# Chunks 0 and 1 of a feed-forward stage: other order of VectorE and ScalarE work, other PSUM banks for the first transposed x, two memsets earlier

## The chip, the core and the metric

The kernel runs on one core of a Trainium2 chip. Five engines share the work: TensorE (PE in the rows, its weight loads PEld), VectorE (DVE), ScalarE (ACT), GpSimd (POOL) and SyncE (SP), which issues every DMA here. Each works through its own instructions in order and waits on semaphores. The metric is the device time of one execution in microseconds (us), lower is better. Before the change it is 366.3 us, the median of three runs (364.39 to 366.59).

## What is computed

For x of shape (16, 256, 256) in float32:

```python
xn = _layernorm(x, axis=-1)
x = x + _L0_attn_ref(xn, w_qkv, w_out) + _L0_ffn_ref(xn, w_gating, w_linear)

# _L0_ffn_ref: every product takes float8 (e4m3) inputs
ff_gate = _qdot(x, w_gating[0])          # 256 -> 1024
gate_value = jax.nn.gelu(ff_gate)
ff1 = _qdot(x, w_gating[1])
activations = gate_value * ff1
outputs = _qdot(activations, w_linear)   # 1024 -> 256
```

The attention has 16 heads of 16, a causal mask and softmax, in float32.

## The kernel before

The 4096 rows of x are worked as 8 chunks of 512 tokens in a feed-forward (FFN) stage, about the first 110 us; after it a long attention stage runs over the 16 batches. In the profile of the kernel before the FFN of chunk c, called "chunk c" here, starts on TensorE at 10.78 us for chunk 0, then at 25.53, 37.76, 49.50 and 61.25 us for the chunks 1 to 4.

Layernorm of a chunk: VectorE takes statistics of four tiles (`find_stats`, L369), joins them (`aggregate`, L378), GpSimd raises the variance to the power -1/2 (`find_rstd`, L288 and L290), VectorE writes the normalised tiles `xn` (`normalize`, L387, four of 128x256). `xn` is a single buffer. TensorE transposes it (`transpose_x`, L661, twice four of 128x128) into two PSUM banks `xt_ps`. ScalarE reads each bank twice: `cast_xt` (L516) makes the fp8 input `x8` of the products, `round_xt` (L521) the high float32r part of a copy that attention needs. VectorE subtracts the two (`split_xt`, L394) for the low part. SyncE then stores both parts, the tile `xt_part`, to memory (`store_xt`, L188, two DMAs of 512 KB). `xt_part` is a single buffer too, so `round_xt` of chunk c waits on the semaphore `xt_stored` until the stores of chunk c-1 have landed.

The FFN of a chunk has eight steps j. A step is two fp8 matmuls for the gate (L676) and two for the up product (L682), the gelu on ScalarE (L527) and the product of both on VectorE (`activate`, L423). The gate of step j waits for the gelu of step j-2, the up product for the activate of step j-2, since both have two banks. Between the steps of chunk c, TensorE computes a piece of the down product of chunk c-1 (`down`, L697); the first piece of chunk 0 waits for all eight activates and for four casts of `w_linear`.

The weights arrive as float32 by DMA into `arena` and are cast to fp8: the first half of the columns of `w_gating` in one VectorE cast (L406), the second half by VectorE (up, L431) and ScalarE (gate, L596, 1024 elements), `w_linear` (`wl8`) in four ScalarE casts (L600). GpSimd also clears two constants for attention (L300, L301), scales the query weights (`w_raw`, L310), and adds the FFN output to x (`add_ffn`, L298).

What stands between the steps on each engine is written out by hand as conditions on (c, j) in one loop per engine. SyncE issues in order: `store_xt(0)`, then the loads of the attention weights (L193, L194) and of further x (L168), then `store_xt(1)` and so on.

## Time and profile before

| what | value |
|---|---|
| median of three runs | 366.3 us |
| the profiled execution | 366.19 us |
| its span, first to last instruction | 364.5 us |
| TensorE busy | 341.3 us (94%) |
| VectorE busy | 298.5 us (82%) |
| ScalarE busy | 227.6 us (62%) |
| GpSimd busy | 168.2 us (46%) |
| TensorE's share of the chain that ended last | 81% |
| mean granted TensorE clock | 0.972 of 2.4 GHz |

The span leaves out 1.7 us ahead of the first and behind the last instruction. Busy shares are means over stages that differ; the change touches only work between 0 and some 50 us, so those stretches have to be read by themselves. Times in rows are us from the span's start.

### The profile page before, as it was taken

The numbers are of one execution on the slowest core, as the hardware profiler recorded it, in microseconds if no ns is written. First come the engines' busy times: TensorE is split into PE (matmuls) and PEld (weight loads), VectorE is DVE, ScalarE is ACT, GpSimd is POOL, SyncE is SP. The second block draws the span as 40 slices with busy tenths as digits, with TensorE's granted clock in tenths as the row PEclk, the third lists the DMA queues.
The fourth block names the chain that finished last, engine by engine and source line by source line (L and its number), as shares of the span: only waits on it lengthen the run. The fifth ranks groups of instructions, "written<-read, shape, count | busy, mean of one in ns | idle before, by whom it ended". The sixth has DMA issues, their size and how long they took to land.

```text
span 364.5 us, 9751 instructions
## 1 busy us (share of the span) xinstructions
PE 341.3 (94%) x3498; PEld 260.1 (71%) x3498; DVE 298.5 (82%) x1356; ACT 227.6 (62%) x368; POOL 168.2 (46%) x204
## 2 busy tenths in 40 slices
PE   7789999999999789999999999999999999979775
PEld 6336565666677678788788888888887888866454
DVE  5968988998425678999989999999999899996643
ACT  1655786667655376776676767766766767664540
POOL 2212333232235137456665575475566555753441
PEclk9969999999999999999999999999999999995889
DMA  7987655773248242534637528447355373250001
GB/s 251 323 287 224 183 151 141 175 232 123 77 142 298 65 145 90 201 120 150 193 112 225 167 97 263 120 144 246 104 179 195 112 222 118 91 206 30 32 29 59
DMA packets 46553, 57.59 MB, mean 158 GB/s; under 512 B 2664, under 2 KB 39080, under 8 KB 46504
## 3 DMA queue, kind: packets, MB, share of 16 engines
q1 hardware_dynamic: 46504, 56.96, 48.6%
q8 instruction: 28, 0.46, 0.5%
q14 instruction: 21, 0.17, 0.1%
HBM read 16.78 MB, written 12.58 MB: 81 GB/s over the span
## 4 chain that ended last, share of the span: by engine, by line
PE 81%; DVE 10%; ACT 3%; issue 2%; DMA 2%; SPq 0%; POOL 0%; DVEq 0%; ACTq 0%; POOLq 0%
PE ps L805 13%; PE ps L710 12%; PE ps L786 12%; PE ps L765 9%; PE ps L717 7%; PE ps L697 6%; PE ps L676 6%; PE ps L822 6%; PE ps L682 6%; DVE masked L457 3%; PE ps L814 2%; DMA xres<-in_L_attn_x_dram 2%; PE ps L661 2%; ACT arena L572 2%; DVE act L423 1%
## 5 line engine op out<-in xcount | busy, mean ns | idle before, releaser
L457 DVE CUSTOM_DVE_ANT_0 masked<-ps,causal 128x256 bf16<-128x256 f32 (+1 forms) x512 | 148.5, 353 | 21.1 <-PE ps L765 21.1
L572 ACT ACTIVATE arena<-ps 128x1024 f32<-128x1024 f32 x96 | 98.4, 1025 | 61.1 <-PE ps L786 61.0
L330 POOL TENSOR_SCALAR_AFFINE_SELECT arena<-arena 128x512 f32<-128x512 f32 (+1 forms) x96 | 73.6, 787 | 39.1 <-ACT arena L572 38.9
L304 POOL TENSOR_TENSOR qk_part<-w_raw,qk_part 128x512 fp32r<-128x512 f32 x32 | 41.1, 1286 | 55.5 <-ACT qk_part L551 55.5
L527 ACT ACTIVATE gate<-ps 128x512 bf16<-128x512 f32 x64 | 38.5, 602 | 35.0 <-PE ps L676 32.6
L786 PE MATMUL ps<-stack 64*128 64x256 f32 (+1 forms) x512 | 53.0, 307 | 4.8 <-ACT arena L572 4.8
L805 PE MATMUL ps<-arena,v_aug 128*32 128x256 f32 (+1 forms) x1024 | 50.8, 341 | 2.9 <-DVE o_norm L474 2.8
L710 PE MATMUL ps<-xs,wq_part 128*128 128x256 f32 x384 | 52.3, 285 | 0.3 <-ACT w_raw L545 0.3
L765 PE MATMUL ps<-stack 63*128 63x256 f32 (+1 forms) x512 | 48.3, 288 | 3.2 <-DVE row_max L457 3.1
L786 PEld LDWEIGHTS ps<-stack 64*128 64x128 f32 x512 | 36.9, 190 | 18.7 <-issue 7.3
L710 PEld LDWEIGHTS ps<-xs,wq_part 128*128 128x128 f32 x384 | 47.5, 189 | 1.6 <-ACT w_raw L545 0.6
L805 PEld LDWEIGHTS ps<-arena,v_aug 128*32 128x32 f32 x1024 | 30.1, 113 | 19.4 <-issue 6.0
L457 DVE DVE_READ_ACCUMULATOR2_ANT row_max<- 128x1 f32 x512 | 42.3, 83 | 0.0
L765 PEld LDWEIGHTS ps<-stack 63*128 63x128 f32 x512 | 37.4, 191 | 6.9 <-DVE row_max L457 2.4
L298 POOL TENSOR_TENSOR xres<-xres,ffn 128x512 f32<-128x512 f32 x16 | 18.5, 1154 | 37.6 <-ACT ffn L533 37.6
L423 DVE TENSOR_TENSOR arena<-ps,gate 128x512 fp8e4<-128x512 f32 x32 | 22.0, 686 | 16.0 <-ACT gate L527 15.9
L335 POOL TENSOR_TENSOR xt_part<-xn,xt_part 128x256 fp32r<-128x256 f32 x32 | 23.4, 731 | 22.9 <-ACT xt_part L581 22.9
L822 PE MATMUL ps<-wq_part,xt_part 128*128 128x256 f32 x192 | 31.4, 302 | 1.0 <-DVE w_raw L487 1.0
L466 DVE STREAM_TRANSPOSE ps<-ps 128x512 f32<-128x512 f32 x32 | 23.4, 731 | 8.0 <-PE ps L805 8.0
L822 PEld LDWEIGHTS ps<-wq_part,xt_part 128*128 128x128 f32 x192 | 25.5, 195 | 3.8 <-DVE w_raw L487 1.2
L423 DVE TENSOR_TENSOR act<-ps,gate 128x512 fp8e4<-128x512 f32 x32 | 21.9, 684 | 7.2 <-ACT gate L527 4.4
L717 PE MATMUL ps<-wq_part,xs 128*128 128x256 f32 x192 | 26.7, 288 | 0.0
(60 smaller groups left out, 458.6 us busy)
## 6 DMA issues: line engine op xcount, KB each, us to landing
stack<-qk_part SPq DMA_DIRECT2D x96, 256.0 KB, 2.7
xt_store<-xt_part SPq DMA_DIRECT2D x16, 512.0 KB, 4.2
xs<-xt_store SPq DMA_DIRECT2D x16, 512.0 KB, 4.2
out_dram<-w_raw SPq DMA_DIRECT2D x16, 256.0 KB, 4.1
xres<-in_L_attn_x_dram SPq DMA_DIRECT2D x7, 512.0 KB, 6.7
arena<-in_L_ffn_w_gating_dram SPq DMA_DIRECT2D x2, 1024.0 KB, 8.9
stack<-zeros SPq DMA_DIRECT2D x4, 512.0 KB, 7.5
arena<-in_L_ffn_w_linear_dram SPq DMA_DIRECT2D x1, 1024.0 KB, 12.9
```

The lines of the kernel that those rows point to most:

```text
L304: nc.gpsimd.tensor_tensor(qk_part[:, g, QLO:KLO + 1:3, :], qk_raw[:, g, :, :], qk_part[:, g, QHI:KLO, :].bitcast(F32), ALU.subtract).then_ ...
L330: nc.gpsimd.affine_select(diag, diag, pattern=[[0, 1024 // width], [1, P]], compare_op=ALU.is_ge, fill=0.0, base=0, channel_multiplier=-1) ...
L423: nc.vector.tensor_tensor(act8[c % 2][:, j, :], up_ps[j % 2], gate[:, j % 2, :], ALU.mult, saturate=False).then_inc(act_done, 1)
L457: last = nc.vector.tensor_tensor_reduce(masked[:, place, i * width:(i + 1) * width], max_ps[:, place, i * width:(i + 1) * width], causal[: ...
L527: nc.scalar.activation(gate[:, j % 2, :], gate_ps[j % 2], ACT.Gelu_apprx_tanh).then_inc(gelu_done, 1)
L572: nc.scalar.activation(arena[:, n, :, :], exp_ps, ACT.Exp).then_inc(exp_done, 1)
L710: last = nc.tensor.matmul(misc[:, 1, s * S:(s + 1) * S], wq_part[:, a, kt, col:col + P], xs[b % 2][:, z, kt, :], start=(i == 0), stop=(i = ...
L717: last = nc.tensor.matmul(misc[:, 0, t * D:(t + 1) * D], xs[b % 2][:, z, kt, t * P:(t + 1) * P], wq_part[:, a, kt, 2 * D:3 * D], start=(i ...
L765: last = nc.tensor.matmul(max_ps[:, (2 * unit + u) % 3, i * width:(i + 1) * width], st[rows, j0 + i, 0, qt * P:(qt + 1) * P], st[rows, j0 ...
L786: last = nc.tensor.matmul(exp_ps[:, u, i * width:(i + 1) * width], st[rows, j0 + i, 1, kt * P:(kt + 1) * P], st[rows, j0 + i, 0, kt * P:S] ...
L805: last = nc.tensor.matmul(pv_ps[32 * i:32 * i + 32, u * S + kt * P:(u + 1) * S], va[:, kt, 2 * (HG * c + i) + u, :], cols, start=(kt == 0) ...
L822: last = nc.tensor.matmul(misc[:, 0, t * D:(t + 1) * D], ot_part[:, z, c, t * P:(t + 1) * P], wq_part[:, a, c, 3 * D:4 * D], start=(c == t ...
```

## The change

Seven things are altered, all of them around chunks 0 and 1, with a tail in chunk 2:

1. GpSimd clears `zeros` and `v_aug2` before `find_rstd(0)` instead of after `find_rstd(1)`.
2. The first half of `w_gating` is cast by VectorE in two pieces of 256 columns, and the gate of step 2 waits for the second; ScalarE's part of the second half is cast in two pieces of 512 elements, after steps 1 and 2 instead of all after step 1.
3. The transposed x of chunk 0 goes to `exp_ps`, the banks of the down product. The transposes of chunk 1 therefore no longer wait for `split_xt` of chunk 0, and the first down piece does.
4. VectorE in chunk 0: `aggregate(1)` after step 0, its weight cast after step 1, `normalize(1)` in pairs after steps 2 and 3, `split_xt(0)` after steps 4 and 5; `find_stats(2)` and `aggregate(2)` leave chunk 0 for chunk 1.
5. ScalarE in chunk 0: `round_xt(0)` after steps 0 and 3, `cast_xt(1)` after 5 and 6, `w_linear` casts after 3, 4 and two after 7; `round_xt(1)` moves into chunk 1, after its steps 0 and 1.
6. Chunk 1: `normalize(2)` after steps 3 and 4 (before: 0 to 3), the transposes of chunk 2 after the down pieces of steps 5 and 6 (before: 4 and 5), `cast_xt(2)` after 6 and 7; the second halves of `round_xt(2)` and `split_xt(2)` fall into chunk 2.
7. TensorE transposes chunk 1 in one go after step 5 of chunk 0 (before: after 4 and 5).

From chunk 3 on nothing is altered. The core of the diff:

```diff
+            nc.gpsimd.memset(zeros[:, :], 0.0).then_inc(v_ones, 1)
+            nc.gpsimd.memset(v_aug[2][:, :, :, :], 1.0).then_inc(v_ones, 1)
             find_rstd(0)
             find_rstd(1)
...
-            nc.gpsimd.memset(zeros[:, :], 0.0).then_inc(v_ones, 1)
-            nc.gpsimd.memset(v_aug[2][:, :, :, :], 1.0).then_inc(v_ones, 1)
...
+                    if c == 0:
+                        if j == 0:
+                            aggregate(1)
+                        if j == 1:
+                            half = slice(HID // 2, HID)
+                            dve.wait_ge(wg_in[1], 16)
+                            nc.vector.tensor_copy(wg8[:, 1, :, half], wg_raw[:, 1, :, half], saturate=False).then_inc(wg_cast[1], 1)
+                        if j in (2, 3):
+                            normalize(1, 2 * j - 4)
+                            normalize(1, 2 * j - 3)
+                        if j in (4, 5):
+                            split_xt(0, j - 4)
+                        continue
+                    if c == 1:
+                        if j in (0, 1):
+                            find_stats(2, 2 * j)
+                            find_stats(2, 2 * j + 1)
+                        if j == 1:
+                            aggregate(2)
+                        if j == 2:
+                            for k in range(KD):
+                                split_xt(1, k)
+                        if j in (3, 4):
+                            normalize(2, 2 * j - 6)
+                            normalize(2, 2 * j - 5)
...
+                        if j == 7:
+                            aggregate(3)
+                            split_xt(2, 0)
+                        continue
+                    if c == 2 and j == 0:
+                        split_xt(2, 1)
...
+                    if c == 1 and j in (0, 1):
+                        round_xt(1, j)
+                    if c == 1 and j in (6, 7):
+                        cast_xt(2, j - 6)
+                    if c == 1 and j == 7:
+                        round_xt(2, 0)
+                    if c == 2 and j == 0:
+                        round_xt(2, 1)
...
-                if c >= 1:
+                if c >= 2:
                     pe.wait_ge(xt_lo, KD * (c - 1) + k + 1)
...
+                if c == 0 and j == J // 4:
+                    pe.wait_ge(wg_cast[0], 2)
```

How the rows stand in the engines' programs is shown at two places. First ScalarE around the border of chunks 0 and 1, from the gelu of step 5 of chunk 0 (before) and from the same step (after). `CAST arena<-ps` is `cast_xt(1)`, `CAST xt_part` is `round_xt`, `CAST wl` the weight cast, `ACTIVATE gate` the gelu. Before:

```order
L527 ACTIVATE gate<-ps 128x512 [waits act_done,gate_ready]
L600 CAST wl<-arena 128x512 [waits wl_in]
L516 CAST arena<-ps 128x512 [waits xt_ready]
L527 ACTIVATE gate<-ps 128x512 [waits act_done,gate_ready]
L600 CAST wl<-arena 128x512 [waits wl_in]
L516 CAST arena<-ps 128x512 [waits xt_ready]
L521 CAST xt_part<-ps 128x512 [waits xt_stored]
L527 ACTIVATE gate<-ps 128x512 [waits act_done,gate_ready]
L600 CAST wl<-arena 128x512 [waits wl_in]
L521 CAST xt_part<-ps 128x512
```

After:

```order
L559 ACTIVATE gate<-ps 128x512 [waits act_done,gate_ready]
L548 CAST arena<-ps 128x512 [waits xt_ready]
L559 ACTIVATE gate<-ps 128x512 [waits act_done,gate_ready]
L548 CAST arena<-ps 128x512 [waits xt_ready]
L559 ACTIVATE gate<-ps 128x512 [waits act_done,gate_ready]
L634 CAST wl<-arena 128x512 [waits wl_in] x2
L559 ACTIVATE gate<-ps 128x512 [waits act_done,gate_ready]
L553 CAST xt_part<-ps 128x512 [waits xt_stored]
L559 ACTIVATE gate<-ps 128x512 [waits act_done,gate_ready]
L553 CAST xt_part<-ps 128x512
```

The cast that waits on `xt_stored` moved from behind step 6 of chunk 0 to behind step 0 of chunk 1; the next gelu in the queue behind it is now that of step 1 of chunk 1.

Second VectorE at the same border, from the activate of step 7 of chunk 0. `TENSOR_TENSOR act` and `arena` are activates, `xt_part` is `split_xt`, `TENSOR_SCALAR xn` is `normalize`. Before:

```order
L423 TENSOR_TENSOR act<-ps,gate 128x512 [waits up_ready,gelu_done]
L394 TENSOR_TENSOR xt_part<-ps,xt_part 128x512 [waits xt_hi]
L423 TENSOR_TENSOR arena<-ps,gate 128x512 [waits up_ready,gelu_done]
L387 TENSOR_SCALAR xn<-xres,mean_var,rstd 128x256 [waits xt_ready,rstd_done]
L423 TENSOR_TENSOR arena<-ps,gate 128x512 [waits up_ready,gelu_done]
L387 TENSOR_SCALAR xn<-xres,mean_var,rstd 128x256
L423 TENSOR_TENSOR arena<-ps,gate 128x512 [waits up_ready,gelu_done]
L387 TENSOR_SCALAR xn<-xres,mean_var,rstd 128x256
```

After, from the activate of step 0 of chunk 1:

```order
L427 TENSOR_TENSOR arena<-ps,gate 128x512 [waits up_ready,gelu_done]
L373 BN_STATS stats<-xres 128x6 [waits x_in1]
L373 BN_STATS stats<-xres 128x6
L427 TENSOR_TENSOR arena<-ps,gate 128x512 [waits up_ready,gelu_done]
L373 BN_STATS stats<-xres 128x6 x2
L382 BN_AGGR mean_var<-stats 128x2 [waits stats_step]
L382 BN_AGGR mean_var<-stats 128x2 x3
L427 TENSOR_TENSOR arena<-ps,gate 128x512 [waits up_ready,gelu_done]
L398 TENSOR_TENSOR xt_part<-ps,xt_part 128x512 [waits xt_hi] x2
L427 TENSOR_TENSOR arena<-ps,gate 128x512 [waits up_ready,gelu_done]
L391 TENSOR_SCALAR xn<-xres,mean_var,rstd 128x256 [waits xt_ready,rstd_done]
L391 TENSOR_SCALAR xn<-xres,mean_var,rstd 128x256
```

The statistics of chunk 2 and their aggregate now stand in chunk 1, ahead of its normalize, which starts behind step 3 instead of step 0.

## Rows read from the trace of the kernel before

**Rows 1.** The profile page: its first line.

```profile
span 364.5 us, 9751 instructions
```

**Rows 2.** Busy time of each engine by stretch, with granted TensorE clock and DMA share.

```profile
core 0: us, PE busy (x) PEld busy (x) DVE busy (x) ACT busy (x) POOL busy (x), PEclk, DMA share, GB/s
10.78:25.53 14.75, 11.46 (x42) 4.85 (x40) 11.58 (x30) 8.43 (x16) 2.43 (x4) 0.77 0.90 289
25.53:37.76 12.23, 11.46 (x72) 7.07 (x73) 9.97 (x24) 8.33 (x17) 4.13 (x5) 1.00 0.77 227
37.76:49.50 11.74, 11.61 (x74) 7.00 (x72) 10.80 (x25) 8.62 (x18) 3.56 (x5) 1.00 0.64 181
61.25:97.00 35.75, 35.75 (x226) 21.66 (x223) 31.13 (x66) 25.34 (x50) 10.50 (x12) 1.00 0.47 135
```

**Rows 3.** Timeline of TensorE: start, duration, line, operation, [idle before, releaser].

```profile
10.78 0.59 PE L676 MATMUL ps<-x,wg 128*128 128x512 fp8e4 x2
11.21 0.59 PE L682 MATMUL ps<-x,wg 128*128 128x512 fp8e4 x2
...
15.96 0.60 PE L682 MATMUL ps<-x,wg 128*128 128x512 fp8e4 x2 [1.81 <-DVE act L423]
...
19.32 1.12 PE L661 MATMUL ps<-ident,xn 128*128 128x128 f32 x4 [0.80 <-DVE xn L387]
...
25.53 0.60 PE L676 MATMUL ps<-arena,wg 128*128 128x512 fp8e4 x2 [0.17 <-ACT arena L516]
...
32.99 0.60 PE L661 MATMUL ps<-ident,xn 128*128 128x128 f32 x4
```

**Rows 4.** Timeline of VectorE in chunk 0.

```profile
13.32 0.69 DVE L431 CAST wg<-arena 128x1024 fp8e4<-128x1024 f32 x1 [0.27 <-DMA arena<-in_L_ffn_w_gating_dram]
14.09 1.22 DVE L387 TENSOR_SCALAR xn<-xres,mean_var,rstd 128x256 f32<-128x256 f32 x1
...
17.34 0.68 DVE L394 TENSOR_TENSOR xt_part<-ps,xt_part 128x512 fp32r<-128x512 f32 x1
17.94 0.40 DVE L387 TENSOR_SCALAR xn<-xres,mean_var,rstd 128x256 f32<-128x256 f32 x1
18.26 0.68 DVE L423 TENSOR_TENSOR act<-ps,gate 128x512 fp8e4<-128x512 f32 x1
```

**Rows 5.** Timeline of ScalarE in chunk 0.

```profile
18.01 0.61 ACT L600 CAST wl<-arena 128x512 fp8e4<-128x512 f32 x1
...
25.36 0.60 ACT L521 CAST xt_part<-ps 128x512 fp32r<-128x512 f32 x1
25.84 0.62 ACT L527 ACTIVATE gate<-ps 128x512 bf16<-128x512 f32 x1
```

**Rows 6.** Timeline of GpSimd.

```profile
14.22 0.94 POOL L301 MEMSET v_aug<- 128x1024 f32 x1
...
26.05 1.04 POOL L290 TENSOR_TENSOR rstd<-var_eps,minus_half 128x4 f32<-128x4 f32 x1
27.19 1.51 POOL L310 TENSOR_SCALAR w_raw<-w_raw 128x512 f32<-128x512 f32 x1
33.48 1.15 POOL L298 TENSOR_TENSOR xres<-xres,ffn 128x512 f32<-128x512 f32 x1 [4.78 <-ACT ffn L533]
```

**Rows 7.** Timeline of SyncE's queue, two rows.

```profile
3.40 0.74 SPq L181 DMA_DIRECT2D arena<-in_L_ffn_w_linear_dram  x1
...
18.05 1.31 SPq L188 DMA_DIRECT2D xt_store<-xt_part  x2
```

**Rows 8.** DMA: page (last number: us to landing); chunk 0's two stores, from issue.

```profile
arena<-in_L_ffn_w_linear_dram SPq DMA_DIRECT2D x1, 1024.0 KB, 12.9
...
DMA to landing us min/median/max: 3.4/4.1/4.8
```

**Rows 9.** Busy time by stretch, the columns of rows 2: around the fall of the clock.

```profile
13.10:17.48 4.38, 2.07 (x9) 0.62 (x9) 4.09 (x7) 2.40 (x4) 2.06 (x3) 0.98 0.99 315
17.50:24.00 6.50, 5.70 (x17) 2.88 (x18) 4.37 (x10) 2.81 (x6) 0.00 (x0) 0.50 0.75 229
```

More of the change, by code:

```diff
@@ L404, in _ @@
             dve.wait_ge(wg_in[0], 16)
-            half = slice(0, HID // 2)
-            nc.vector.tensor_copy(wg8[:, :, :, half], wg_raw[:, :, :, half], saturate=False).then_inc(wg_cast[0], 1)
+            for i in range(2):
+                cols = slice(i * HID // 4, (i + 1) * HID // 4)
+                nc.vector.tensor_copy(wg8[:, :, :, cols], wg_raw[:, :, :, cols], saturate=False).then_inc(wg_cast[0], 1)
             for i in range(CT):
                 find_stats(1, i)
-            aggregate(1)
             def split_wq(i, k):
@@ L590, in _ @@
                     gelu(c, j)
[L591 to L593 removed]
+                    if c == 0 and j in (0, 3):
+                        round_xt(0, j // 3)
+                    if c == 0 and j in (1, 2):
                         half = slice(HID // 2, HID)
                         act.wait_ge(wg_in[1], 16)
[L596 to L598 removed]
+                        nc.scalar.copy(wg8[:, 0, j - 1, half], wg_raw[:, 0, j - 1, half], saturate=False).then_inc(wg_cast[1], 1)
+                    if c == 0 and j in (5, 6):
+                        cast_xt(1, j - 5)
+                    for i in {(0, 3): (0,), (0, 4): (1,), (0, 7): (2, 3)}.get((c, j), ()):
+                        rows = slice(2 * i, 2 * i + 2)
                         act.wait_ge(wl_in, 16)
                         nc.scalar.copy(wl8[:, rows, :], wl_raw[:, rows, :], saturate=False).then_inc(wl_cast, 1)
+                    if c == 1 and j in (0, 1):
[6 more added lines that the diff above has]
+                        round_xt(2, 1)
                     if c >= 2 and j == 0:
@@ L692, in down @@
                         pe.wait_ge(wl_cast, J // 2)
+                        pe.wait_ge(xt_lo, KD)
                 if piece % 4 == 0 and c >= 1:
```

40 lines of the change are left out of this document (19 added, 21 removed).

## Prediction

> **What bounds the kernel now.** I read the stretches first. The span is 364.5 us [rows 1] of the execution's 366.19, so 1.69 us lie outside it; the execution is 0.1 us under the median of 366.3. From chunk 4 on TensorE is busy 35.75 of 35.75 us at the full clock [rows 2]: there its own matmuls are the bound, and any time that TensorE wins or loses in chunks 0 to 2 is carried to the end unchanged. Chunk 1 takes 12.23 us with 11.46 busy, chunk 2 11.74 with 11.61, so 0.8 us of idle time is all that those two hold. Chunk 0 takes 14.75 us with a mean clock of 0.77 [rows 2]. Its work is short: the matmuls for one gate or one up product start 0.43 us apart (10.78 and 11.21 [rows 3]), eight steps are 7.0 us, with the two transposes 7.8. So chunk 0 holds about 7 us that are not TensorE's own.
>
> Then the timeline of TensorE. It sits idle 1.81 us before 15.96 and 0.80 us before 19.32 [rows 3], behind VectorE. VectorE's first normalize of chunk 1 takes 1.22 us at 14.09 [rows 4] against 0.40 for one at 17.94; it ends at 15.31, just after GpSimd's memset of 14.22 + 0.94 = 15.16 [rows 6]. Of the stretch 13.10 to 17.48 TensorE is busy 2.07 us out of 4.38, and in 17.50 to 24.00 the granted clock is 0.50, the lower level of 1.2 GHz [rows 9].
>
> **The change, step by step.** I carry the new orders forward with the spacings of the rows: on ScalarE a gelu or cast starts 0.48 us after the one before it (25.36, 25.84 [rows 5]), a weight cast about the same; on VectorE an activate or split takes 0.60 and a normalize 0.32 (17.34, 17.94, 18.26 [rows 4]); a result is used about 0.04 us after it is there.
>
> Chunk 0. The memsets, now ahead of the first rstd, run while VectorE awaits x; nothing waits for them. If they delayed VectorE's own memsets, the cost is 0 to 0.6 us at the start, and it would vanish in the two DMA waits below; I take 0. TensorE starts at 10.78 as before. The activate of step 1 no longer stands behind rstd(1), so steps 0 to 3 run without a stall until 14.2. The second half of `w_gating` lands at 13.3 (VectorE's cast at 13.32 [rows 4]), ScalarE's two pieces end about 15.0, and step 4 starts there. `w_linear` was issued at 3.40 [rows 7] and takes 12.9 us to land [rows 8]: 16.3. ScalarE now wants it at 15.8 (before: at 18.01 [rows 5]), a stall of 0.5, so the gelu of step 4 starts at 16.9. From there ScalarE does four gelus (steps 4 to 7), two `cast_xt` and three weight casts, nine times about 0.49: the gelu of step 0 of chunk 1 starts at 21.3 (before: 25.84 [rows 5]). TensorE transposes chunk 1 at 17.1 (before 19.32 [rows 3]), at the full clock, and opens chunk 1 at 20.0 (before 25.53 [rows 3]). Chunk 0 has won 5.6 us.
>
> The new wait. `split_xt(0)` has moved from steps 1 and 2 to steps 4 and 5 of VectorE. Before, its second half ended at 17.34 + 0.68 = 18.02, and SyncE issued the two stores at 18.05, 1.31 us together [rows 7]. Now: gelu 4 at 16.9, activate 4 at 17.5, split 18.1, activate 5 at 18.7, split 19.3 to 20.0. SyncE issues at 20.05 and 20.7, and the later store lands 4.8 us after its issue [rows 8]: 25.5. Before, that was 23.5, and `round_xt(1)` came only at 25.36 [rows 5], so it waited for nothing. Now ScalarE reaches `round_xt(1)` at 21.8, right behind its first gelu of chunk 1, and stands until 25.6: 3.8 us. Behind it in ScalarE's queue is the gelu of step 1, now at 26.1, behind that the activate of step 1 (26.8) and, by the two gate banks, TensorE's gate of step 3. TensorE computes steps 0 to 2 and is idle from 24.5 to 26.8. Before, step 3 lay two steps of 1.30 (gate, up, down piece, 0.43 each) ahead of the transposes at 32.99 [rows 3], at 30.4, so 3.6 us of the lead are still there.
>
> The late statistics. Only behind the activate of step 1 do the last statistics and `aggregate(2)` follow: they end at 28.6, and GpSimd's two steps (0.3 and 1.04 [rows 6]) give rstd(2) at 30.1 (before 26.05 + 1.04 = 27.1). VectorE comes to `normalize(2)` behind the activate of step 3 at 30.9. GpSimd then scales `w_raw`, 1.51 us from 30.0, and adds the FFN result, 1.15 us [rows 6], since copy_ffn is done by 30.3; the weights for the scaling are there at 29.2 (27.19 less 18.05 [rows 6, 7] behind the new issue at 20.05). These two ran at 27.19 and 33.48, clear of each other. Rows 4 show what a normalize does beside GpSimd: it ended 0.15 us behind a memset that started after it, so it was held over two GpSimd instructions. So the first normalize of chunk 2 ends at 32.8, the last at 34.4, with the activate of step 4 between, and the transposes of chunk 2, at 32.99 before [rows 3], start at 34.4, 1.4 us later. TensorE is idle from 32.0 to 34.4. This port has a rule: the Trainium skill, page SBUF — State Buffer, section SBUF: two separate sides, has VectorE and GpSimd share one pair of ports under an exclusive lock, held for one whole instruction by whoever starts first. By it normalize could slip in between the scaling and the addition; the transposes would start near 34.1 and the sum below would be 0.3 us less. The row with 1.22 us speaks for the longer hold.
>
> Then less is left to do than before at that point, as the transposes stand a step later: one of them, two steps, two down pieces, the other, 3.5 us, but `cast_xt(2)` comes only after the gelu of step 7, and chunk 2 opens at 38.4 instead of 37.76 [rows 2]: 0.6 us late. In chunk 2 the second `split_xt(2)` stands ahead of the first normalize of chunk 3, 0.6 us more on VectorE; TensorE's wait for that chunk's `xn`, small before (chunk 2 held 0.13 us idle [rows 2]), grows by 0.5. Together +1.1 us. From chunk 3 all is as before.
>
> The clock. TensorE is busy 3.9 us (at full speed) out of the 9.9 between 24.5 and 34.4, less than the 2.07 of 4.38 behind which it fell to 1.2 GHz before [rows 9]. A fall is likely. Where it costs is open: the low level began near 17.3 (the mean of 0.98 up to 17.48 leaves 0.2 us for it) and held at least to 24.0 [rows 9], some 7 us; between 24.5 and 34.4 TensorE waits for others and half speed hides; dense work behind 34.4 pays half of the low time. Lower end 0, if it recovers by 34.4; upper end 3.5 if all 7 us fall behind it. By the nearest row, the fall came about 1.3 us after the end of the idle time (15.96 to 17.3): here 28.1 to 35.1, so 0.7 us of dense work at half speed, a loss of 0.35. I take +0.4.
>
> Sum: 366.2 + 0.6 + 0.5 + 0.4 = 367.7 us. The low clock of chunk 0, 7 us long, is gone, but it wins nothing more: its end lay ahead of the store's landing.
>
> **Rivals.** (a) The clock falls late: the same stalls, but TensorE pays 1.2 to 3.5 us of it behind 34.4: 368.5 to 370.8. For it: two idle stretches of 2.3 us and the second right ahead of dense work. Against it: one fall may be over by then. It decides from 34.4 us on. (b) The store is early enough. Were xt_stored there when ScalarE comes, chunk 1 would shift by 2.6 us: 366.2 - 1.5 = 364.7. For it: the first of the two stores took 3.4 us, not 4.8 [rows 8]; a landing 1.1 us sooner would already give 366.7. Against it: the wait needs the second store as well. More than 3.7 us, a gain of over 1%, asks that also rstd(2) and the normalizes come free of GpSimd, for which no row speaks: chunk 2 would open near 34. (c) The losses cancel the gain to within 0.7 us: chunk 1 is bound by its own chain (statistics, rstd, normalize), and a few tenths less there (the port, rule above) end at 366.2.
>
> **Numbers.** My case, 367.0 to 368.5: 0.42. Rival (a): 0.25. (b): 0.17. (c): 0.16. The range must hold 0.8: from 364.6, the fully hidden wait, to 370.4, most of (a). This kernel's measurement tells about 1% (3.7 us) from no change. Slower by more than that (over 370.0) is the upper part of (a), 0.13 with what is unforeseen; faster (under 362.6) is the far end of (b), 0.05; within 1% 0.82.
>
> **What would show it.** In the profile of the changed kernel: TensorE's gates of step 3 at about 13.4 without idle time, opening chunk 1 at about 20; ScalarE idle some 3.8 us in front of the `round_xt` of chunk 1, ended by a DMA, near 25.6; VectorE's first normalize of chunk 2 near 31 with over 1 us duration; TensorE idle twice over 2 us between 24 and 35; chunk 2 opening at 38 to 39. Wrong would be: no ScalarE stall there, or a chunk 2 that opens before 36.5; and a granted clock of 0.5 behind 35 us would move the result to (a).

## The result, and the profile after

| | before | after |
|---|---|---|
| median | 365.25 us (6 executions, 361.95 to 366.59) | 368.59 us (6 executions, 366.66 to 370.12) |
| profiled execution | 366.19 us | 367.46 us |
| span | 364.5 us | 365.7 us |
| mean granted TensorE clock | 0.972 | 0.981 |

The ratio of after to before is 1.0087, with a 95% interval of 1.0051 to 1.0122: the change makes the kernel some 3 us slower. A few executions of a kernel run one or two per cent slower at a lower granted clock; the ratios here and below leave them out and are worked out from all the others, so they are not exactly the quotients of the medians. The predicted time was 367.7 us in a range of 364.6 to 370.4.

The page of the changed kernel, its first two lines and the chain that ended last:

```profile
span 365.7 us, 9753 instructions
...
PE 340.6 (93%) x3498; PEld 258.6 (71%) x3498; DVE 297.9 (81%) x1357; ACT 227.5 (62%) x369; POOL 169.0 (46%) x204
...
PE 73%; DVE 12%; DMA 5%; issue 4%; ACT 3%; SPq 1%; POOL 1%; DVEq 0%; ACTq 0%
```

The chain of the kernel before:

```profile
PE 81%; DVE 10%; ACT 3%; issue 2%; DMA 2%; SPq 0%; POOL 0%; DVEq 0%; ACTq 0%; POOLq 0%
```

No engine has more or less to do. What changed is the chain: TensorE's share fell from 81% to 73%, and that of DMAs rose from 2% to 5%. Where that lies, the stretches show; the first three are the chunks 0, 1 and 2, the fourth is as long as the last one of [rows 2], and the last two are cut around TensorE's waits:

```profile
core 0: us, PE busy (x) PEld busy (x) DVE busy (x) ACT busy (x) POOL busy (x), PEclk, DMA share, GB/s
10.96:21.02 10.06, 8.72 (x40) 3.46 (x41) 9.06 (x23) 7.81 (x16) 1.83 (x2) 1.00 0.78 263
21.02:38.87 17.85, 14.03 (x74) 7.24 (x73) 12.29 (x29) 8.42 (x17) 3.97 (x4) 0.90 0.78 247
38.87:51.11 12.24, 11.54 (x73) 7.00 (x74) 11.19 (x29) 8.87 (x18) 3.99 (x5) 1.00 0.76 201
62.85:98.60 35.75, 35.75 (x226) 21.67 (x223) 31.12 (x66) 25.39 (x50) 10.49 (x12) 1.00 0.46 135
24.00:28.00 4.00, 1.91 (x14) 1.09 (x12) 0.52 (x3) 1.26 (x3) 0.00 (x0) 1.00 0.93 288
28.80:32.00 3.20, 3.20 (x11) 1.47 (x10) 2.86 (x10) 1.28 (x4) 1.63 (x3) 0.50 0.63 219
```

Against [rows 2], chunk 0 takes 10.06 us instead of 14.75, chunk 1 17.85 instead of 12.23, chunk 2 12.24 instead of 11.74, and the dense chunks the same 35.75. Chunk 1 opens 4.51 us earlier than before and gives 5.62 us back, so chunk 2 opens 1.11 late and chunk 3 1.61 (51.11 against 49.50). Chunk 0 now runs at the full clock; the low level of 1.2 GHz is found from 28.8 to 32.0.

Then TensorE's timeline, to set beside [rows 3]:

```profile
10.96 0.60 PE L720 MATMUL ps<-x,wg 128*128 128x512 fp8e4 x2
...
13.72 0.60 PE L726 MATMUL ps<-x,wg 128*128 128x512 fp8e4 x2 [0.42 <-DVE act L427]
...
16.06 0.60 PE L720 MATMUL ps<-x,wg 128*128 128x512 fp8e4 x2 [0.87 <-ACT wg L628]
...
21.02 0.60 PE L720 MATMUL ps<-arena,wg 128*128 128x512 fp8e4 x2
...
27.88 0.60 PE L720 MATMUL ps<-arena,wg 128*128 128x512 fp8e4 x2 [2.09 <-ACT gate L559]
...
34.87 0.66 PE L703 MATMUL ps<-ident,xn 128*128 128x128 f32 x4 [0.95 <-DVE xn L391]
...
38.87 0.60 PE L720 MATMUL ps<-x,wg 128*128 128x512 fp8e4 x2 [0.30 <-ACT x L548]
...
46.28 0.66 PE L703 MATMUL ps<-ident,xn 128*128 128x128 f32 x4 [0.70 <-DVE xn L391]
```

The two long waits for VectorE in chunk 0 (1.81 and 0.80 in [rows 3]) are gone; the up product of step 2 still waits 0.42 us, and the gate of step 4 waits 0.87 us for ScalarE's cast. In chunk 1 there are two new ones: 2.09 us until the gelu of step 1 frees a gate bank, and 0.95 us for `xn` of chunk 2. The last row is the wait for `xn` of chunk 3, which chunk 2 did not show before.

ScalarE, against [rows 5], and the two stores in SyncE's queue with their landing, against [rows 7, 8]:

```profile
14.38 0.62 ACT L628 CAST wg<-arena 128x512 fp8e4<-128x512 f32 x1 [1.19 <-DMA arena<-in_L_ffn_w_gating_dram]
...
17.39 0.62 ACT L634 CAST wl<-arena 128x512 fp8e4<-128x512 f32 x1 [0.41 <-DMA arena<-in_L_ffn_w_linear_dram]
...
26.74 0.59 ACT L553 CAST xt_part<-ps 128x512 fp32r<-128x512 f32 x1 [3.75 <-DMA xt_store<-xt_part]
27.22 0.60 ACT L559 ACTIVATE gate<-ps 128x512 bf16<-128x512 f32 x1
```

```profile
21.05 2.61 SPq L192 DMA_DIRECT2D xt_store<-xt_part  x2
...
DMA to landing us min/median/max: 4.2/4.6/5.0
```

ScalarE stands 3.75 us in front of the `round_xt` of chunk 1, where before it waited for nothing. The gelu at 27.22 is the one that TensorE's row at 27.88 names. VectorE and GpSimd, against [rows 4, 6]:

```profile
20.34 0.68 DVE L398 TENSOR_TENSOR xt_part<-ps,xt_part 128x512 fp32r<-128x512 f32 x1
...
27.86 0.69 DVE L427 TENSOR_TENSOR arena<-ps,gate 128x512 fp8e4<-128x512 f32 x1 [3.48 <-ACT gate L559]
...
32.33 1.01 DVE L391 TENSOR_SCALAR xn<-xres,mean_var,rstd 128x256 f32<-128x256 f32 x2
...
33.86 0.96 DVE L391 TENSOR_SCALAR xn<-xres,mean_var,rstd 128x256 f32<-128x256 f32 x2
...
45.82 0.40 DVE L391 TENSOR_SCALAR xn<-xres,mean_var,rstd 128x256 f32<-128x256 f32 x1
```

```profile
30.51 1.04 POOL L294 TENSOR_TENSOR rstd<-var_eps,minus_half 128x4 f32<-128x4 f32 x1
31.64 1.56 POOL L314 TENSOR_SCALAR w_raw<-w_raw 128x512 f32<-128x512 f32 x1
33.17 1.18 POOL L304 TENSOR_TENSOR xres<-xres,ffn 128x512 f32<-128x512 f32 x1
...
45.86 1.38 POOL L304 TENSOR_TENSOR xres<-xres,ffn 128x512 f32<-128x512 f32 x1 [3.56 <-ACT ffn L565]
```

The chain of waits between 20 and 40 us puts these rows in one line; its columns are start, duration, and what it was:

```profile
20.34 0.69 DVE xt_part L398
...
21.05 0.64 SPq L192
...
21.73 4.98 DMA xt_store<-xt_part
...
27.22 0.61 ACT gate L559
...
27.86 0.69 DVE arena L427
...
32.33 1.01 DVE xn L391 x2
...
34.87 0.66 PE ps L703 x4
```

Read downwards: the second `split_xt(0)`, the issue of the second store, its flight of 4.98 us, the gelu that stood behind `round_xt`, VectorE's activate, statistics and normalizes of chunk 2, and only then TensorE. From 26.7 to 34.8 nothing in this chain is TensorE's.

### The profile page after: what moved, and what is told of

It is laid out like the page before. It is cut to its first block, busy times and chain, and to the rows that moved or that the text cites. A ratio compares the mean times of both kernels' runs of the same rounds, so it can differ in the third digit from the quotient of the medians.

```text
span 365.7 us, 9753 instructions
## 1 busy us (share of the span) xinstructions
PE 340.6 (93%) x3498; PEld 258.6 (71%) x3498; DVE 297.9 (81%) x1357; ACT 227.5 (62%) x369; POOL 169.0 (46%) x204
## 4 chain that ended last, share of the span: by engine, by line
PE 73%; DVE 12%; DMA 5%; issue 4%; ACT 3%; SPq 1%; POOL 1%; DVEq 0%; ACTq 0%
PE ps L856 12%; PE ps L756 12%; PE ps L837 11%; PE ps L816 8%; PE ps L763 6%; PE ps L743 5%; PE ps L720 5%; PE ps L873 5%; PE ps L726 4%; DVE masked L489 4%; DMA xres<-in_L_attn_x_dram 3%; PE ps L865 2%; ACT arena L604 2%; PE ps L703 2%; DVE xn L391 2%
## 5 line engine op out<-in xcount | busy, mean ns | idle before, releaser
L756 PE MATMUL ps<-xs,wq_part 128*128 128x256 f32 x384 | 53.4, 289 | 0.3 <-ACT w_raw L577 0.3
L756 PEld LDWEIGHTS ps<-xs,wq_part 128*128 128x128 f32 x384 | 48.5, 192 | 1.6 <-ACT w_raw L577 0.6
L873 PE MATMUL ps<-wq_part,xt_part 128*128 128x256 f32 x192 | 30.5, 296 | 1.0 <-DVE w_raw L519 1.0
L873 PEld LDWEIGHTS ps<-wq_part,xt_part 128*128 128x128 f32 x192 | 24.6, 189 | 3.7 <-DVE w_raw L519 1.2
L763 PE MATMUL ps<-wq_part,xs 128*128 128x256 f32 x192 | 26.7, 288 | 0.0
```

The lines of the kernel that those rows point to most:

```text
L756: last = nc.tensor.matmul(misc[:, 1, s * S:(s + 1) * S], wq_part[:, a, kt, col:col + P], xs[b % 2][:, z, kt, :], start=(i == 0), stop=(i = ...
L763: last = nc.tensor.matmul(misc[:, 0, t * D:(t + 1) * D], xs[b % 2][:, z, kt, t * P:(t + 1) * P], wq_part[:, a, kt, 2 * D:3 * D], start=(i ...
L873: last = nc.tensor.matmul(misc[:, 0, t * D:(t + 1) * D], ot_part[:, z, c, t * P:(t + 1) * P], wq_part[:, a, c, 3 * D:4 * D], start=(c == t ...
```

## The experiments

Two theories stood at the start. The first: chunk 0's gain is real, and the wait of ScalarE for the store of `xt_part` takes it away. The rival: chunk 1 is bound by its own chain of statistics, rstd and normalize, with GpSimd's two instructions beside it, so that the store only looks guilty. Every kernel below computes the whole reference. Ratios are to the kernel before, timed on the same chip; "opens" is the first gate of a chunk on TensorE in the profiled execution, in us. Chips differ: the median of the kernel before was 365.43 for the kernels e, 365.55 for f, 365.82 for g and 365.88 for h1, so kernels of different letters are compared by their ratios. This is the table of all of them:

| kernel | chunk 1 opens | chunk 2 | chunk 3 | median us | ratio [95%] |
|---|---|---|---|---|---|
| before | 25.53 | 37.76 | 49.50 | 365.25 | 1 |
| after | 21.02 | 38.87 | 51.11 | 368.59 | 1.0087 [1.0051, 1.0122] |
| e0_after_again | 20.74 | 40.07 | 52.31 | 369.67 | 1.0139 [1.0091, 1.0186] |
| e1_buffer | 20.73 | 34.47 | 46.71 | 363.91 | 0.9974 [0.9944, 1.0005] |
| e2_scale_waits | 20.80 | 39.48 | 51.72 | 369.25 | 1.0114 [1.0070, 1.0158] |
| e3_buffer_scale_waits | 21.09 | 34.82 | 47.07 | 364.25 | 0.9974 [0.9944, 1.0003] |
| f1_split_early | 20.61 | 37.18 | 50.36 | 367.53 | 1.0040 [1.0012, 1.0068] |
| f2_split_late | 20.82 | 40.39 | 52.64 | 370.29 | 1.0119 [1.0080, 1.0157] |
| f3_round_late | 21.15 | 35.69 | 48.87 | 367.44 | 1.0048 [1.0015, 1.0082] |
| f4_before_memsets | 22.53 | 34.94 | 46.68 | 365.04 | 0.9974 [0.9943, 1.0005] |
| g1_memsets_back | 21.72 | 39.23 | 52.41 | 370.48 | 1.0140 [1.0096, 1.0185] |
| g2_buffer_old_banks | 22.52 | 36.78 | 49.96 | 369.65 | 1.0104 [1.0044, 1.0163] |
| g3_before_again | 26.14 | 38.37 | 50.12 | 366.36, one execution | none |
| h1_buffer_pool_waits | 20.41 | 34.16 | 45.70 | 362.72 | 0.9918 [0.9882, 0.9955] |

One caution for reading it: from the first gate of chunk 7 to the end, where all these kernels are alike, the profiled executions take between 268.0 and 270.7 us of their spans, so a single span is uncertain by over 1 us in either direction. The openings tell where time goes, the medians tell how much is left at the end. The two do not agree in size: e1, e3 and f4 open chunk 3 2.79, 2.43 and 2.82 us before the kernel before does, and their ratio of 0.9974 is 1.0 us; the changed kernel opens it 1.61 us late and is 3 us slower. In every row the ratio lies 0.6 to 3.3 us above what the openings say, and why is not shown.

**The changed kernel once more.** No edit; it is the base for its neighbours on that chip.

> The changed kernel unaltered, beside the three edits of it that follow, for comparison on one chip. All theories: the ratio to the kernel before lies in the interval measured, 1.005 to 1.012, and ScalarE stands some 3.8 us in front of the first round_xt of chunk 1.

Measured: ratio 1.0139, above the interval of the first measurement, though the two intervals overlap. ScalarE's row and the landing of the two stores:

```profile
27.95 0.59 ACT L553 CAST xt_part<-ps 128x512 fp32r<-128x512 f32 x1 [5.24 <-DMA xt_store<-xt_part]
...
DMA to landing us min/median/max: 3.3/4.9/6.5
```

The stores were issued at 20.78, 0.27 earlier than in the first profile, yet the later one landed 6.5 us after its issue instead of 5.0. The stall is 5.24 us and chunk 2 opens 1.20 us later. The length of the stall differs from one execution of the same program to the next.

**A second buffer.** The transposed x of chunk 1 goes to memory that lies unused then, so its `round_xt` need not await chunk 0's store; order and work are those of the changed kernel.

```diff
+        xt_spare = stack[3][:, :, :, :].rearrange("p j a s -> p (j a s)")[:, 0:2 * KD * C].rearrange("p (a k t) -> p a k t", a=2, k=KD)
+
+        def xt_of(c):
+            return xt_spare if c == 1 else xt_part
...
-                if c >= 1 and k == 0:
+                if c >= 2 and k == 0:
...
-                nc.scalar.copy(xt_part[:, 0, k, :], xt_ps(c, k)).then_inc(xt_hi, 1)
+                nc.scalar.copy(xt_of(c)[:, 0, k, :], xt_ps(c, k)).then_inc(xt_hi, 1)
```

> The changed kernel with a second buffer for the xt_part of chunk 1 (it lies in stack[3], unused until much later), so that round_xt(1) needs no wait for the stores of chunk 0. Theory S (the store's landing): ScalarE's 3.8 us of waiting are gone, TensorE's gate of step 3 of chunk 1 comes 2.1 to 2.3 us earlier, the transposes of chunk 2 2.6 us earlier, and the time falls by 2.6 us against the changed kernel, ratio to before about 1.002 or a bit below. Theory P (GpSimd's scaling and addition beside normalize, with the late statistics): chunk 1 ends no earlier, since rstd(2) and the port hold it; ratio stays near 1.009. Theory C (a late fall of the clock costs most): the idle 2.1 us of TensorE at 25.8 are gone, so the fall is rarer; a gain too, but the profile would show the low clock in the changed kernel behind 35 us and not here.

Measured: 363.91 us against 369.67 on the same chip, 5.8 us less, and 0.9974 of before, with an interval that reaches 1.0005: level with it or a little faster. The gain is over twice the 2.6 us expected. Rows of ScalarE, VectorE and TensorE:

```profile
22.54 0.63 ACT L559 CAST stack<-ps 128x512 fp32r<-128x512 f32 x1
...
28.45 0.73 DVE L397 TENSOR_SCALAR xn<-xres,mean_var,rstd 128x256 f32<-128x256 f32 x2
...
34.47 0.60 PE L726 MATMUL ps<-x,wg 128*128 128x512 fp8e4 x2 [0.30 <-ACT x L554]
```

The cast that came at 26.74 or 27.95 comes at 22.54, without a wait, and chunk 2 opens 4.4 us earlier than in the first profile of the changed kernel and 5.6 earlier than in the second. From the opening of chunk 1 to that of chunk 2 it takes 13.74 us, where those two took 17.85 and 19.33: 4.11 and 5.59 less, each time the stall (3.75 and 5.24) and 0.35 us more, and the first pair of normalizes takes 0.73 instead of 1.01. So the wait for the store is the cause, and chunk 1 pays its full length. The stall itself grew between the forecast (3.8) and this comparison (5.24); the forecast of 2.6 had also let the stall move what follows by less than its length.

**GpSimd out of the way.** The scaling of the query weights waits for the last normalize of chunk 2, first in the changed kernel, then in the one with the second buffer.

```diff
+                    pool.wait_ge(xn_done, 3)
                     pool.wait_ge(wq_in, 32)
```

> The changed kernel; GpSimd waits for the last normalize of chunk 2 before it scales the query weights, so that neither this nor the addition behind it runs beside a normalize of chunk 2. Theory S: 1.5 us of the loss at most are the port's, since the first two normalizes took 1.01 us and the other two 0.96 where a pair takes 0.72 alone: by those rows 0.5 us less, by the prediction's own working (held over both instructions) 1.5 us; ratio 1.004 to 1.008. Theory P: the port is the larger part, 1.5 us or more, ratio 1.004 or lower. A price: the scaling comes later, at about 34.5 us, still ahead of its first reader at 41 us.

> Both edits together. If the store's wait and the port each hold chunk 1 by themselves, the parts add: carrying the orders forward, chunk 2 opens 5.0 us earlier than in the changed kernel (2.6 for the wait, 2.4 for the port, which without the stall would collide with the normalizes more than with it), so 3.9 us less than before, ratio to before 0.989 to 0.993. Theory S alone: like the buffer alone, 1.002. Theory P alone: like the scale alone. Theory C: the two stretches of idle time of over 2 us on TensorE are gone and with them the fall of the clock, 1.0 throughout chunks 1 and 2.

Measured: 1.0114 for the first, above the 1.004 to 1.008 expected; but its base on that chip is 1.0139, and beside that the difference lies within the intervals. The openings are finer. The pair of normalizes takes its unhindered time:

```profile
33.46 0.73 DVE L392 TENSOR_SCALAR xn<-xres,mean_var,rstd 128x256 f32<-128x256 f32 x2
```

From the end of the stall to the opening of chunk 2 it is 11.61 us (27.87 to 39.48), against 12.13 in the changed kernel (26.74 to 38.87) and 12.12 in its second profile. The shared port is worth 0.5 us there. The second kernel was expected at 0.989 to 0.993 if the parts added; it gives 0.9974, the same as the buffer alone: with the buffer alone the scaling comes only when its weights have landed, at 30.11, when the first pair is done and the second (29.70) is under way; the pairs take 0.73 and 0.72, so nothing was left to win at that place. The rival falls: without the store's wait the chain of chunk 1 is ready 4.4 us sooner.

**The store earlier or later.** `split_xt(0)` one step earlier, behind steps 3 and 4 of chunk 0 (the diff), or in the same way one step later, behind 5 and 6.

```diff
-                        if j in (4, 5):
-                            split_xt(0, j - 4)
+                        if j in (3, 4):
+                            split_xt(0, j - 3)
```

> The changed kernel with split_xt(0) one step earlier, after steps 3 and 4 of chunk 0 instead of 4 and 5. Theory S (the time hangs on when the stores of chunk 0 are issued): VectorE's second split ends about 1.1 us sooner (19.7 instead of 20.7 or 21.0), SyncE issues the stores so much sooner, ScalarE's stall in front of round_xt(1) shrinks from 3.8 to 5.2 us by as much, and the time falls by about 1.1 us against the changed kernel, ratio near 1.009 where it was 1.0114 to 1.0139 on the last chip. Rival D (the landing is set by what else is in the DMA queues, not by the issue): the stall ends when it did, near 27 to 28 us, and the time stays.

> The changed kernel with split_xt(0) one step later, after steps 5 and 6 of chunk 0. Theory S: the stores are issued some 0.6 to 1.2 us later (an activate and what it waits for stand between), and the time grows by as much, 0.6 to 1.2 us. Rival D: no change.

Measured: the issue of the stores and ScalarE's wait, of the early kernel and then of the late one:

```profile
19.53 1.31 SPq L192 DMA_DIRECT2D xt_store<-xt_part  x2
...
25.07 0.58 ACT L553 CAST xt_part<-ps 128x512 fp32r<-128x512 f32 x1 [2.49 <-DMA xt_store<-xt_part]
```

```profile
21.86 1.31 SPq L192 DMA_DIRECT2D xt_store<-xt_part  x2
...
28.28 0.59 ACT L553 CAST xt_part<-ps 128x512 fp32r<-128x512 f32 x1 [5.50 <-DMA xt_store<-xt_part]
```

Issue at 19.53, 20.78 or 21.05, and 21.86 gives a stall of 2.49, 5.24 or 3.75, and 5.50 us, and ratios of 1.0040, 1.0139 or 1.0087, and 1.0119. The early store is clearly faster. The late one can't be told from the changed kernel by its time (0.6 to 1.2 us more was expected); its stall ends at 28.28, after 27.95 and 26.74. So the earlier side is shown. It also rules out the rival that the landing is set by the other DMAs whatever the time of issue: there the stall would have ended near 27 to 28 us, and it ended at 25.07. The early kernel wins 2.9 us at the opening of chunk 2 against e0, but only 1.95 at that of chunk 3: its chunk 2 takes 13.18 us instead of 12.24, of which more below.

**The waiting cast two steps later.** `round_xt(1)` behind steps 2 and 3 of chunk 1 and both halves of `split_xt(1)` behind step 3; the store stays where the change put it.

```diff
-                    if c == 1 and j in (0, 1):
-                        round_xt(1, j)
+                    if c == 1 and j in (2, 3):
+                        round_xt(1, j - 2)
...
-                        if j == 2:
+                        if j == 3:
```

> The changed kernel with only the place of round_xt(1) altered: after the gelus of steps 2 and 3 of chunk 1 instead of 0 and 1 (and split_xt(1) after the activate of step 3 instead of 2). No second buffer, the wait stays. Theory S: the cast still waits until the stores land at 27 to 28 us, but ScalarE reaches it at 25.2 instead of 22.5, with two more gelus behind it, so that what is queued behind is the gelu of step 3 instead of step 1: two steps, 2.6 us, are won back, ratio about 1.005. It cannot win more than the second buffer did (5.8 us). Rival P (statistics and port bind chunk 1): aggregate(2) then comes earlier too, so it would win the like; told apart only by f1 and f2. Rival D: as theory S.

Measured: 1.0048. The stall shrinks to 0.78 us and chunk 2 opens at 35.69, 3.2 us earlier than in the changed kernel. It too has a chunk 2 of 13.18 us. The stall ends at 26.46, 0.28 earlier than in the changed kernel, but ScalarE has done two more gelus meanwhile: what made the wait dear was its place in ScalarE's queue.

**The memsets alone.** The two memsets ahead of the first rstd in the kernel before, and behind the second one in the changed kernel.

```diff
+            nc.gpsimd.memset(zeros[:, :], 0.0).then_inc(v_ones, 1)
+            nc.gpsimd.memset(v_aug[2][:, :, :, :], 1.0).then_inc(v_ones, 1)
             find_rstd(0)
             find_rstd(1)
-            nc.gpsimd.memset(zeros[:, :], 0.0).then_inc(v_ones, 1)
-            nc.gpsimd.memset(v_aug[2][:, :, :, :], 1.0).then_inc(v_ones, 1)
```

> The kernel before with only the two memsets moved ahead of find_rstd(0). By the rows of before the first normalize of chunk 1 took 1.22 us beside them and 0.40 without, on VectorE's chain to the activate and to TensorE: 0.6 to 0.85 us less if the low clock of chunk 0 stays, up to 2.3 us less if the shorter idle time also spares it (replayed at full clock chunk 2 opens at 35.5 instead of 37.8); ratio 0.994 to 0.998. Rival: the memsets now delay VectorE's own memsets and the first statistics by up to 0.6 us, and nothing is won, ratio 1.000 or above.

> The changed kernel with the two memsets put back behind find_rstd(1). They would then run at about 16.0 to 17.3 us, beside the first pair of normalizes of chunk 1 (16.14 in the changed kernel). By the 1.22 us of that row in the kernel before, the pair is held some 1.2 us, and with it every later step of VectorE in chunk 0, the second split_xt(0) and the issue of the stores: theory S wants the store issued near 22.2, ScalarE released near 28.5 to 29, and the time up by 1.0 to 1.2 us against the changed kernel. Rival: the shift is hidden by the stall that follows, and the time stays.

Measured: in the kernel before, the first normalize of chunk 1 takes 0.41 us instead of 1.22, chunk 1 opens 3.0 us and chunk 2 2.8 us earlier; ratio 0.9974. In that execution the clock did not fall either (1.00 in chunks 0 and 1), and the profile does not separate what the shorter wait gave from what the clock gave. By the ratio 1.0 us is left and by the medians 0.5, with an interval that reaches to no change. In the changed kernel the memsets in their old place make a pair of normalizes take

```profile
16.25 1.49 DVE L391 TENSOR_SCALAR xn<-xres,mean_var,rstd 128x256 f32<-128x256 f32 x2
```

instead of 0.72, chunk 1 opens 0.7 us later, and the store's wait swallows most of it: chunk 2 opens 0.36 us later than in the first profile of the changed kernel. The ratio is 1.0140 beside 1.0139 for e0: in the changed kernel the earlier memsets give nothing that can be measured, where 1.0 to 1.2 us were expected.

**The banks alone.** The kernel with the second buffer, with the first transposed x in its old banks, so that the transposes of chunk 1 wait for `split_xt(0)` again.

```diff
-                return exp_ps[:, k, :] if c == 0 else misc[:, k, :]
+                return misc[:, k, :]
...
-                if c >= 2:
+                if c >= 1:
                     pe.wait_ge(xt_lo, KD * (c - 1) + k + 1)
```

> The changed kernel with the second buffer, and with the transposed x of chunk 0 back in the banks misc, so that the transposes of chunk 1 wait again for split_xt(0). What the part with the PSUM banks is worth, now that the stall does not cover it: the transposes of chunk 1 must wait until VectorE's splits at 19.5 and 20.7, where they ran at 17.9; cast_xt(1) and the gate of step 0 of chunk 1 follow 1.5 to 2 us later, and the time is 1.0 to 2.0 us above that of the buffer alone (ratio 1.000 to 1.003 where that had 0.9974). Rival: VectorE, not TensorE, bounds chunk 1 in that kernel, and the two match within 0.5 us.

Measured: 1.0104, beside 0.9974 for the same kernel with the new banks. TensorE waits

```profile
19.16 0.63 PE L709 MATMUL ps<-ident,xn 128*128 128x128 f32 x4 [1.85 <-DVE xt_part L404]
```

and chunk 1 opens 1.8 us later, chunk 2 2.3, chunk 3 3.25. Only the 1.8 are the banks' own: 0.5 is from the normalizes of chunk 1, which now meet GpSimd (pairs of 1.01 and 0.96), and 0.94 is again a long chunk 2. That is why the ratio lies above the 1.000 to 1.003 expected. With `split_xt(0)` as late as the change puts it, the other banks are needed.

**The kernel before once more.** No edit, one execution, to tell whether its low clock in chunk 0 was an accident.

> One more profile of the kernel before, for two things that two profiles leave open. First, whether the low clock of chunk 0 (0.50 from 17.3 to 24.0 us) comes in every execution: if so, chunk 2 opens near 37.8; if the clock stays at 1.00, near 36.3 by the same orders at full speed, and the span is about 1.4 us shorter. Second, when the second half of w_gating lands: 13.3 and 13.1 us in the two profiles of the old order, 14.0 to 14.6 in all eight of the new. If that belongs to the program it lands near 13.2 here, if to chance it may land at 14.

Measured: 366.36 us, with the low level again from 17 to 24 us and chunk 1 opening at 26.14. So it stands in both profiles of that kernel. The landing of the second half of `w_gating` is 13.93 us here and 13.32 in the first profile of the same program, so chance alone moves it by 0.6. The eleven profiles of the changed order have it between 13.56 and 14.57, f4 at 13.07. The ranges overlap, and whether the order has a part in it is not settled.

**All additions of GpSimd behind the normalizes.** In f1, f3, g1 and g2 chunk 2 takes 13.18 us, in all others above of the changed order 12.24 or 12.25. The rows of VectorE and of GpSimd in f1 show why, to be set beside those of the changed kernel at 45.82 and 45.86:

```profile
44.14 1.33 DVE L391 TENSOR_SCALAR xn<-xres,mean_var,rstd 128x256 f32<-128x256 f32 x1
```

```profile
44.17 1.15 POOL L304 TENSOR_TENSOR xres<-xres,ffn 128x512 f32<-128x512 f32 x1 [3.55 <-ACT ffn L565]
```

The last normalize for chunk 3 and an addition of GpSimd start within 40 ns of each other. In the changed kernel the normalize took 0.40 and the addition 1.38; here the normalize took 1.33 and the addition 1.15. One of the two is held, and TensorE waits for the one, not for the other. The last kernel adds to the second buffer a wait that keeps them apart in every chunk:

```diff
             for c in range(CHUNKS):
+                if 1 <= c <= CHUNKS - 2:
+                    pool.wait_ge(xn_done, c + 2)
```

> This is e1_buffer (the changed kernel with a second tile for the transposed x of chunk 1), and one wait more: from chunk 1 on GpSimd starts its work of a chunk (the addition of the FFN output, the scaling of the query weights, the two steps to rstd) only when VectorE has written the last normalised tile for the next chunk. It asks whether GpSimd's additions that fall beside the normalizes cost anything. In e1_buffer and in the changed kernel the first normalize of most chunks takes 1.06 to 1.11 us instead of 0.40, and the last normalize and the addition of chunk 2 start within 40 ns of each other, now the one held and now the other. Theory (the shared port costs time on the path): every normalize takes 0.40, chunk 2 takes about 11.5 us between its first gate and that of chunk 3 (12.24 in e1_buffer, 13.18 where VectorE is the one held), chunk 3 about 11.4 (11.74), the sum is about 1 us less than e1_buffer: ratio to the kernel before 0.992 to 0.996. Rival (the hold is hidden by other work except where the last normalize is hit): chunk 2 stays at 12.24, chunk 3 at 11.74, ratio 0.996 to 0.999, and the only thing won is that 13.18 cannot occur. Second rival: the additions come so late that ScalarE waits for GpSimd with the next FFN output, or the square root power for the next chunk is late: GpSimd's pow ends behind the point where VectorE wants it, idle time of VectorE in front of the first normalize, ratio over 1.000.

Measured: 362.72 us, 0.9918 [0.9882, 0.9955]. The theory's numbers come out: chunk 2 takes 11.54 us, chunk 3 11.44 (11.74 in e1_buffer), and every normalize 0.40 or 0.41. The stretches of chunks 1 and 2, in the columns of [rows 2], and one row each of VectorE and GpSimd in chunk 2:

```profile
20.41:34.16 13.75, 12.17 (x74) 6.78 (x73) 11.68 (x29) 8.53 (x17) 3.90 (x4) 1.00 0.93 293
34.16:45.70 11.54, 11.50 (x72) 7.11 (x73) 10.47 (x29) 9.00 (x18) 3.73 (x5) 1.00 0.87 240
```

```profile
40.41 0.41 DVE L399 TENSOR_SCALAR xn<-xres,mean_var,rstd 128x256 f32<-128x256 f32 x1
```

```profile
40.90 2.27 POOL L310 TENSOR_TENSOR xres<-xres,ffn 128x512 f32<-128x512 f32 x2 [4.75 <-DVE xn L399]
```

VectorE is busy 10.47 us in chunk 2 instead of 11.19 in the changed kernel, and TensorE idles 0.04 us there instead of 0.70. The openings of chunk 3 differ from those of e1_buffer by 1.01 us, of which 0.31 lay ahead of chunk 2 already. This kernel beats both the one before and the changed one. It was timed on another chip than e1_buffer, and the intervals of the two ratios just overlap, so that it is faster than e1_buffer is shown by the openings and not by the times. Chunk 1 still holds 1.6 us of idle TensorE, so it is not the end of what the new order can give.

## Why the prediction was right, and where it was short

**Chunk 0: right in the main, with a late landing.** The steps 0 to 3 did not run without a stall, as was said: the up product of step 2 waited 0.42 us for the activate of step 0 (13.72), and the gate of step 3 came at 14.16 instead of 13.4. It cost nothing, since step 4 waits for the weights in either case. Step 4 was to start at 15.0 and started at 16.06, because the second half of `w_gating` landed at 14.38, not 13.3; everything behind it is about 1.05 us late: the `w_linear` stall ends at 17.39 (predicted 16.3, length 0.41 against 0.5), chunk 1 opens at 21.02 (20.0). The gain was named as 5.6 us (its own openings give 5.5) and came to 4.5.

**The new wait: right in place and length.** ScalarE stood 3.75 us before `round_xt(1)`, predicted 3.8; it ended at 26.74 (25.6 and the 1.05); the gate of step 3 came at 27.88 (26.8). The store took 4.98 us to land, taken was 4.8.

**The late statistics and the port: place right, one term mis-sized.** `rstd(2)` was ready at 31.55 (30.1 and 1.05 would be 31.15). The normalizes started at 32.33 (30.9 and 1.05 is 31.95). But the step "it was held over two GpSimd instructions" failed. It priced the hold at 1.5 us. Measured is 0.5: the two pairs take 1.01 and 0.96 instead of 0.73. Inside the first pair one normalize takes 0.41 beside the scaling, unheld, and the other 0.70; it ends at 33.34, 0.14 behind the scaling. The first of the second pair ends 0.15 behind the addition. The Trainium skill, page SBUF — State Buffer, section SBUF: two separate sides, says that the engine which has the shared port keeps it for one whole instruction; the prediction gave that reading a gain of 0.3 us and the longer hold the preference. Here VectorE did slip in, so the rule is nearer than the row of 1.22 us. What the rule does not explain is the normalize of 0.41 us that ran while the scaling had been going on for 0.7 us. The error of 1.0 us in this term made up for most of the 1.05 us late landing and the 0.4 us above, and so the transposes of chunk 2 stand at 34.87 against 34.4 and chunk 2 at 38.87 against 38.4: two errors that cancel to a half microsecond, and that is luck.

**Chunk 2: right.** Predicted +0.5, measured 12.24 against 11.74. The cause given was the second `split_xt(2)` ahead of the first normalize. That normalize starts 2.47 us after the opening of chunk 2 (41.34), where before it started 2.03 after (39.79), and was held to 1.11 and 1.06 us beside an addition of GpSimd; the row at 46.28 has the idle time of 0.70 for `xn` as said. h1 adds that this time can be had back by keeping GpSimd away from the normalizes, with the split where it is.

**The clock: seen, but free.** It fell and came back between 28.8 and 32.1, some 3.3 us instead of the seven taken from [rows 9], and in that time no piece of the chain is TensorE's. The term of 0.4 was 0 in this execution, and rival (a) with it. The second idle stretch of over 2 us that was forecast is 0.95 long, as TensorE filled the slack at half speed. The openings give +1.61 us. The prediction's +1.5 was +1.1 of openings and 0.4 of clock: chunk 2 opened 0.5 later than worked out and the clock cost nothing, so that these two nearly agree is luck too.

**The size of the difference: short by half.** The profiled execution took 367.46 us for 367.7. The difference of the medians, though, is 3.3 us, and 4.2 beside e0, not 1.5. Part of this is the starting point: the execution of before from which the sum was made, 366.19, is 0.9 us above that kernel's median of 365.25. Another part may be the store's landing: the sum took 4.8 us from one execution, and the changed kernel, e2 and e0 have 5.0, 6.3 and 6.5, with stalls of 3.75, 5.10 and 5.24 us. Two profiles of the changed kernel, 1.2 us apart at chunk 2, are all there is for this; that the median execution has the longer stall is argued, not shown. And it can't be the whole: e1, e3, f4 and h1, which have no such stall, lie 0.8 to 1.9 us above their openings as well. What is common to all of them was not found. In the changed kernel, e2 and e0 the DMA engines are busy to a share of 0.93 or more while ScalarE waits (24.00 to 28.00 above). SyncE issues the loads of the attention weights and of x right behind the stores, so they share the engines; what makes one landing 1.5 us longer than another was not separated.

**Rival (b) was priced too low.** Were the store early enough, 364.7 us was said, 3.0 less than the forecast. e1 shows 5.8 us less than the changed kernel on that chip. The failing step is "chunk 1 would shift by 2.6 us": from the end of the wait all that follows hangs on it, through gelu, activate, statistics and normalize, so the whole stall moves, and the first pair of normalizes is no longer held. Chunk 1 became 4.11 us shorter than in the changed kernel's first profile. Rival (c) named the right price for the port, some tenths, but not the end of it, since the store ran late.

## What to carry to other kernels

When work that fills a single buffer is moved later, follow the store that empties it to its next user, and count what stands in that user's queue: here one cast that waited held up gelus, statistics and a layernorm that had nothing to do with it. The wait for a DMA on the chain cost its full length here and varied with the landing, 1.5 us between two executions, so a second buffer was worth more than a reordering (the ratio fell from 1.0139 to 0.9974 by the buffer, to 1.0040 by the earlier split, on another chip and with the long chunk 2). Where GpSimd and VectorE both work on float32 in SBUF, place GpSimd's optional work by a wait instead of leaving it to the moment: together with the second buffer that gave the only version clearly faster than before. And an earlier opening in a profile is not yet a faster kernel: 2.8 us at chunk 3 were 1.0 us in the ratio.

## What the runs showed of the hardware

**A tie for the port.** An addition on GpSimd and a normalize on VectorE that start 30 to 50 ns apart end in one of two ways: normalize 0.40 and addition 1.38, or 1.33 and 1.15. In both cases VectorE's start is the earlier one in the trace. Of ten profiles six went the first way (the changed kernel, e0, e1, e2, e3, f2) and four the second (f1, f3, g1, g2), and what decides was not found. It changes the length of chunk 2 by 0.94 us. This bears out the Trainium skill's rule (page SBUF — State Buffer, section SBUF: two separate sides) that one engine holds the port while the other stands; but where VectorE went first its normalize ran 0.36 us beyond the addition's start, and the addition grew by only 0.23.

**Back to back is not always held through.** Two memsets of GpSimd that follow each other without a gap held one normalize to 1.22 us [rows 4, 6] and in g1 a pair to 1.49. A scaling and an addition that follow each other as closely let VectorE through in between (a normalize of 0.70 that ended 0.14 behind the scaling).

**The landing of a load and of a store.** The same load of `w_gating` landed between 13.07 and 14.6 us in the profiles, and the same store between 4.6 and 6.5 us after its issue.

**The clock.** TensorE's granted clock fell to the lower level behind a stretch in which it was busy 1.91 of 4.00 us, as it had behind 2.07 of 4.38 [rows 9]; in f4, with idle pieces of 0.94, 0.48, 1.23, 0.58 and 0.96 us in chunk 0 and the start of chunk 1, it did not fall. Nor did it in chunk 1 of g1, where TensorE was busy 2.11 of the 4.00 us from 25.00 to 29.00, nearly as little.
